# Softmax of the router on 128 partitions, norms two to four units later, another order of the mixers in chunk 0

## What is computed

```python
x = x + _layernorm(_L0_attn_ref(_layernorm(x), a_params, B_w, C_w, D))
x = x + _layernorm(_L0_ffn_ref(_layernorm(x), w_router, w_gating, w_gate, w_up, w_down))

# _L0_attn_ref: Bu = u B_w^T; h = causal convolution of Bu with eig**t, |eig| = 1 (by FFT); y = h C_w^T + D u
# _L0_ffn_ref:
router_probs = softmax(x w_router)
gate_weights = softmax(x w_gating / 0.1)
g, u = x w_gate[e], x w_up[e]          # e = 0..7, 128 -> 512
expert_out = (silu(g) * u) w_down[e]   # 512 -> 128
cw = router_probs * gate_weights
cw = cw / (sum(cw) + 1e-9)
out = sum over e of expert_out[e] * cw[e]
```

## Time and profile before

| | |
|---|---|
| median of 3 runs | 1156.24 us (1155.15 to 1158.2) |
| profiled execution, its time | 1157.83 us |
| profiled execution, its span | 1156.0 us |
| PE, PE weight loads | 1111.9, 898.4 us busy (96%, 78%) |
| DVE | 952.7 us (82%) |
| ACT | 735.2 us (64%) |
| POOL | 721.6 us (62%) |
| DMA | 80.17 MB, mean 69 GB/s |
| granted TensorE clock, mean | 0.996 |

### The profile page before, as it was taken

The page is one execution under the profiler, slowest core; times in us unless marked ns, Lnnn a source line. Parts: engine busy times, 40 slices in busy tenths (PEclk is TensorE's granted clock), DMA queues, the critical chain, the costliest instruction groups (busy, mean ns, idle before and its releaser), DMA issues.

```text
span 1156.0 us, 16762 instructions
## 1 busy us (share of the span) xinstructions
PE 1111.9 (96%) x4818; PEld 898.4 (78%) x4818; DVE 952.7 (82%) x1655; ACT 735.2 (64%) x1415; POOL 721.6 (62%) x900
## 2 busy tenths in 40 slices
PE   7799999999999999999999999999999999999997
PEld 4677787877878778787877878778787877878785
DVE  7778888798898978888897888978888798887865
ACT  6666665756666576675756667576666656656554
POOL 1477765758567475765748566485765748566453
PEclk9999999999999999999999999999999999999998
DMA  4430322313132122322213132222312313132110
GB/s 135 117 101 19 95 62 71 76 46 93 45 92 74 51 79 47 101 56 74 74 46 100 39 93 73 64 67 51 97 55 74 82 39 101 37 83 55 40 53 19
DMA packets 184588, 80.17 MB, mean 69 GB/s; under 512 B 126736, under 2 KB 162224, under 8 KB 184496
## 3 DMA queue, kind: packets, MB, share of 16 engines
q1 hardware_dynamic: 184496, 79.09, 25.7%
HBM read 59.40 MB, written 19.66 MB: 68 GB/s over the span
## 4 chain that ended last, share of the span: by engine, by line
PE 70%; POOL 14%; issue 7%; DVE 7%; ACT 1%; DMA 1%; SPq 0%; POOLq 0%; DVEq 0%; ACTq 0%
PE y L362 8%; PE g L362 7%; PE g L364 7%; PE g L363 7%; PE y L364 7%; PE y L363 7%; PE u L362 7%; PE u L364 7%; PE u L363 7%; POOL hid_lo L1276 6%; POOL acc L1283 3%; DVE e_pos L908 2%; POOL rstd L1248 1%; DVE hid L974 1%; DVE y_part L989 1%
## 5 line engine op out<-in xcount | busy, mean ns | idle before, releaser
L1276 POOL TENSOR_TENSOR hid_lo<-hid,hid_hi 128x512 fp32r<-128x512 f32 x255 | 342.1, 1342 | 338.4 <-ACT hid_hi L670 338.3
L664 ACT ACTIVATE gate<-g 128x512 f32<-128x512 f32 x512 | 304.8, 595 | 325.3 <-PE g L364 325.3
L974 DVE TENSOR_TENSOR hid<-gate,u 128x512 f32<-128x512 f32 x512 | 346.9, 678 | 158.9 <-ACT gate L664 138.4
L670 ACT ACTIVATE hid_hi<-hid 128x512 fp32r<-128x512 f32 x512 | 319.9, 625 | 51.9 <-DVE hid L974 48.1
L980 DVE TENSOR_TENSOR hid_lo<-hid,hid_hi 128x512 fp32r<-128x512 f32 x257 | 237.3, 923 | 0.3
L362 PE MATMUL y<-hid_hi,w_hi 128*128 128x512 f32 x512 | 201.2, 393 | 14.0 <-POOL hid_lo L1276 13.9
L362 PE MATMUL u<-xe_hi,w_hi 128*128 128x512 f32 x512 | 201.4, 393 | 11.4 <-DVE hid L974 11.4
L362 PE MATMUL g<-xe_hi,w_hi 128*128 128x512 f32 x512 | 200.0, 391 | 0.1
L364 PE MATMUL u<-xe_hi,w_lo 128*128 128x512 f32 x512 | 199.6, 390 | 0.0
L364 PE MATMUL y<-hid_hi,w_lo 128*128 128x512 f32 x512 | 199.6, 390 | 0.0
L363 PE MATMUL u<-xe_lo,w_hi 128*128 128x512 f32 x512 | 199.6, 390 | 0.0
(11 more groups left out here) (223 smaller groups left out, 1192.2 us busy)
## 6 DMA issues: line engine op xcount, KB each, us to landing
cw_b<-cw_scratch SPq DMA_DIRECT2D x128, 256.0 KB, 3.4
x_sb<-x_in SPq DMA_DIRECT2D x16, 256.0 KB, 3.1
xn_scratch<-mix_t SPq DMA_DIRECT2D x60, 64.0 KB, 2.7
feat<-xn_scratch SPq DMA_DIRECT2D x15, 256.0 KB, 2.6
out_scratch<-acc_t SPq DMA_DIRECT2D x60, 64.0 KB, 1.9
ffn<-out_scratch SPq DMA_DIRECT2D x15, 256.0 KB, 2.7
x_out<-o_sb SPq DMA_DIRECT2D x15, 256.0 KB, 2.2
y_scratch<-mix_t SPq DMA_DIRECT2D x56, 64.0 KB, 1.9
```

What stands on the lines that cost most here:

```text
L664: nc.scalar.activation(gate[:, k % 2, :], g_ps[k % 2][:], ACT.Silu).then_inc(gate_ready, 1)
L670: nc.scalar.activation(hid_hi[:, k % RING, :], hid[:, k % RING, :], ACT.Copy).then_inc(hi_ready, 1)
L974: nc.vector.tensor_tensor(hid[:, k % RING, :], gate[:, k % 2, :], u_ps[k % 2][:], ALU.mult).then_inc(hid_ready, 1)
L1276: nc.gpsimd.tensor_tensor(hid_lo[:, k % RING, :], hid[:, k % RING, :], hid_hi[:, k % RING, :].bitcast(f32), ALU.subtract).then_inc(lo_pool, 1)
```

## The change

The four tables and a new one for chunk 2's mixers in chunk 0 (`SECOND_X_AT`) move steps between units. In the steady chunks x's first half is two units earlier up to `bu`, y's norm and `z` two units later, the final norm two later. The softmax's tiles have 128 partitions and 4 groups of tokens (128x64 for 32x256). A 32x32 transposition stays within its partitions' block or moves to another; four instructions put the four quarters of the row onto the four blocks of partitions, and four put them back. `lo_x` on DVE waits for `act_hi`, not for `du` that follows it on ACT. In chunk 0 the store of x's blocks goes ahead of `store_cw`, and chunk 1's silus run in chunk 1's unit 0.

```diff
-X_AT = {"load_x": 0, "stats_x": 6, "norm_x": 7, "scale_x_a": 9, "scale_x_b": 10, "block_x": 12, "hi_x": 17, "du": 18,
-        "lo_x": 18, "bu": 20, "enter": 21, "scan": 22, "leave": 23, "hi_w": 25, "lo_w": 26, "c": 28, "y": 29, "block_y": 30}
-Y_AT = {"stats_y": 4, "norm_y": 5, "z_a": 7, "z_b": 8, "residual": 9, "stats_x1": 14, "norm_x1": 15, "scale_x1_a": 17,
...
+X_AT = {"load_x": 0, "stats_x": 4, "norm_x": 5, "scale_x_a": 7, "scale_x_b": 8, "block_x": 10, "hi_x": 15, "du": 16,
+        "lo_x": 16, "bu": 18, "enter": 19, "scan": 21, "leave": 22, "hi_w": 24, "lo_w": 25, "c": 27, "y": 28, "block_y": 30}
+Y_AT = {"stats_y": 6, "norm_y": 7, "z_a": 9, "z_b": 10, "residual": 11, "stats_x1": 14, "norm_x1": 15, "scale_x1_a": 18,
...
-FIN_AT = {"fin_turn": 7, "fin_stats": 10, "fin_norm": 11, "fin_a": 20, "fin_b": 21, "fin_add": 23}
+FIN_AT = {"fin_turn": 7, "fin_stats": 12, "fin_norm": 13, "fin_a": 21, "fin_b": 22, "fin_add": 23}
...
-        lg, e_neg, e_pos = (sb(n, [SMALL, SEQ // SMALL, 2, E]) for n in ("lg", "e_neg", "e_pos"))
+        lg, e_neg, e_pos = (sb(n, [P, NT, 2, E]) for n in ("lg", "e_neg", "e_pos"))
...
             def body(c, par, first, last):
                 if c + 2 < NCHUNK:
                     load_x(c + 2)
+                if first:
+                    store_x_blocks(1)
                 store_cw(c, par)
+                if first:
+                    load_x_feat(1)
                 for e in range(E):
                     spread_cw(c, par, e, first)
-                    if first and e == 0:
-                        store_x_blocks(1)
-                        load_x_feat(1)
...
             def mix_lo_x(c):
-                dve.wait_ge(du_ready, c + 1)
+                dve.wait_ge(act_hi_ready, 2 * c - 1)
...
             def mix_softmax_in(c):
                 dve.wait_ge(logits_ready, c + 1)
-                nc.vector.transpose(sum_sb[0:SMALL, :], n_ps[0:SMALL, :]).then_inc(raw_read, 1)
+                for q in range(P // SMALL):
+                    last = nc.vector.transpose(sum_sb[q * SMALL:(q + 1) * SMALL, 0:P], n_ps[0:SMALL, q * P:(q + 1) * P])
+                last.then_inc(raw_read, 1)
...
-                nc.vector.transpose(cw_t[:], v_sb[0:SMALL, :]).then_inc(cw_t_ready, 1)
+                for q in range(P // SMALL):
+                    last = nc.vector.transpose(cw_t[:, q * P:(q + 1) * P], v_sb[q * SMALL:(q + 1) * SMALL, 0:P])
+                last.then_inc(cw_t_ready, 1)
```

More of the change, by code:

```diff
@@ new lines @@
+Y_AT = {"stats_y": 6, "norm_y": 7, "z_a": 9, "z_b": 10, "residual": 11, "stats_x1": 14, "norm_x1": 15, "scale_x1_a": 18,
+        "scale_x1_b": 19, "block_xe": 20, "hi_xe": 25, "lo_xe": 26, "logits": 28, "softmax": 29, "peak": 30, "silus": 31}
+FIRST_X_AT = {"scale_x_a": 0, "scale_x_b": 1, "block_x": 1, "hi_x": 7, "du": 8, "lo_x": 8, "bu": 10, "enter": 11, "scan": 11,
+              "leave": 13, "hi_w": 14, "lo_w": 14, "c": 16, "y": 17}
+FIRST_Y_AT = {"turn_y": 17, "stats_y": 17, "norm_y": 18, "z_a": 20, "z_b": 21, "residual": 22, "stats_x1": 23, "norm_x1": 24,
+              "scale_x1_a": 26, "scale_x1_b": 27, "turn_xe": 28, "hi_xe": 28, "lo_xe": 28, "logits": 29, "softmax": 30,
+              "peak": 31}
@@ L53 @@
+SECOND_X_AT = {"stats_x": 5, "norm_x": 6, "scale_x_a": 9, "scale_x_b": 10, "block_x": 12, "hi_x": 19, "du": 20, "lo_x": 20,
+               "bu": 21, "enter": 22, "scan": 22, "leave": 23, "hi_w": 25, "lo_w": 26, "c": 28, "y": 29, "block_y": 30}
 OWN_AT = {"exps": 0, "products": 1, "weights": 2}
 FIRST_OWN_AT = {"exps": 1, "products": 1, "weights": 2}
-FIN_AT = {"fin_turn": 7, "fin_stats": 10, "fin_norm": 11, "fin_a": 20, "fin_b": 21, "fin_add": 23}
+FIN_AT = {"fin_turn": 7, "fin_stats": 12, "fin_norm": 13, "fin_a": 21, "fin_b": 22, "fin_add": 23}
@@ L58, in stages @@
 def stages(b):
     if b == 0:
-        return [(1, FIRST_X_AT), (1, FIRST_Y_AT), (2, X_AT)]
+        return [(1, FIRST_X_AT), (1, FIRST_Y_AT), (2, SECOND_X_AT)]
     return [(c, at) for c, at in ((b + 1, Y_AT), (b + 2, X_AT)) if c < NCHUNK]
@@ L717, in body @@
                         mix_silus(0)
+                    if c == 1 and k == 0:
+                        mix_silus(1)
                     for m, at in stages(c):
@@ L930, in mix_weights @@
                 dve.wait_ge(soft_link, at + 2)
-                wide_rows = v_sb[0:SMALL, :].rearrange("p (j q) -> p j q", q=SMALL)
+                wide_rows = v_sb[:, 0:P].rearrange("p (j q) -> p j q", q=SMALL)
                 nc.vector.tensor_tensor(wide_rows[:, :, 0:E], pr[:], wide(den[:], E), ALU.mult).then_inc(cw_ready, 1)
```

9 lines of the change are left out of this document (4 added, 5 removed).

## The result

The changed kernel takes 1148.72 us, the median of four runs (1147.37 to 1149.3), against 1156.03 for the kernel before (1155.15 to 1158.2), measured in turn with it. The ratio is 0.9932, with an interval of 0.9915 to 0.9950. That is 7.3 us less where 27.2 were forecast, and the time lies outside the range of 1119 to 1142. The profiled execution took 1147.37 us, its span was 1145.4.

What follows compares the result with a forecast made beforehand. PE, busy 96% of the span, was taken as the bound, so only its waits could go. 12.6 + 14.1 - 3.0 - 2.0 + 5.5 = 27.2 us off 1156.24 gave 1129.0 us, range 1119 to 1142.

Steps and rivals of the forecast that it cites:

- Loss A: Unit 4, chunks 1 to 15: PE loses 0.84 us waiting for DVE's hid behind the softmax; 12.6 us go.
- Loss B: Unit 8, chunks 1 to 14: PE loses 1.01 us to POOL's queue; goes with Loss A, 14.1 us.
- The cover of the transpositions: Between hid 2 and hid 3: three more transpositions cost PE nothing; without cover 0.2 to 0.4 us a chunk.
- Rival 2: POOL's queue stays the bound, a 1.0 us wait returns at unit 10 or 18 in 13 chunks: 1139; chance 0.17.
- Rival 4: Transpositions far above 1.1 us or DVE late otherwise; Loss A and Loss B stay: 1153; chance 0.04.
- the three signs of being wrong: A wait stays at unit 4; 1 us at Loss B's place or later; PE waits at unit 18 behind feat.
- The 3.0 us of new small waits: New waits from POOL's tight queue in steady chunks: 0.23 us in each of 13; bounds 0 and 1.0 a chunk.
- The feature load: Unit 15: ACT stands 1.5 us or more for feat, just covered at PE's unit 18; 2.0 us over all chunks.
- rival 3: Feature load late in every chunk, each us costing PE one; at 2.6 us late, 1163, slower; chance 0.03.
- Chunk 0: Chunk 0 gives 2.0 us at unit 4, 2.4 at unit 9 and 1.1 right behind; together 5.5 us.
- the two terms: Chunk 0: unit 9's wait for act_lo gives 2.4 us, the lower clock right behind it 1.1.
- The later waits: Chunk 0: later waits for POOL, 3.7 us, change place; taken as equal, 3 us either way.

Runs made afterwards that it cites:

- softmax_only: Kernel before with the softmax alone on 128 partitions, all tables of units as they were; 1146.69 us, ratio 0.9906.
- tables_only: Changed kernel with the softmax back on 32 partitions, the new order of the mixers kept; 1165.04 us, ratio 1.0081.
- quarter_back: Changed kernel with one of the four transpositions of mix_weights, the other three left out and their weights constant; 1135.86 us, ratio 0.9820.
- one_input_products: Changed kernel with pr and den formed by a multiplying reduction that reads one operand; 1141.21 us, ratio 0.9868.
- both_cures: Changed kernel with x's stages up to leave as before, y's statistics at unit 2, its norm and mix_weights at unit 3; 1130.07 us, ratio 0.9771.
- chunk0_as_before: Changed kernel with chunk 0's tables, SP's order there and chunk 1's silus as before; 1148.56 us, ratio 0.9926.
- weights_unit3: Changed kernel with mix_weights in unit 3 instead of 2, behind hid of unit 3; 1148.40 us, ratio 0.9939.
- products_unit0: Changed kernel with mix_products in unit 0 instead of 1, behind mix_exps; 1147.42 us, ratio 0.9926.

## Why the prediction was wrong

**Loss A** was right in place, reason and size: the reciprocal of 128x64 takes 0.545 us (0.54 forecast), `hid` of unit 2 starts 1.47 us earlier in the chunk ("at least 1.2"; the 2.3 called more likely was missed by the 0.98 that `den` took more), and 12.6 us went. softmax_only and tables_only show that it is the softmax alone.

**Loss B** is the step that failed, with some 13 of the 14.1 us that it was to give. The sentence was "Those of `mix_weights` stand behind `hid` 2 and ahead of `hid` 3, which gained at least 1.2 us too, so they cost PE nothing", and after it "With A gone the chain ends at 17.37". To be on time POOL had to start 2.0 us earlier in the chunk than before (12.25 to 10.25, of which that part had 0.2 to spare), so `hid` 3 had to gain some 1.8 to 2.0, not "at least 1.2". It gained 0.99. Two terms took the rest. The transpositions were taken at 0.9 us and took 1.24, above the upper bound of 1.1, since each takes 0.30 and the next starts only behind it. The estimate from the Trainium skill, "VectorE: DVE Perf Modes", section on the TRN2 errata, 0.47 us for three more, was nearer: 1.24 less 0.70 is 0.54. And `den` takes 1.13 us instead of the 0.15 of before, a meeting with POOL that the prediction named for `pr` and did not follow to its neighbour. Taking away either alone (0.93 us by quarter_back, 0.98 by one_input_products) removes nearly all of the wait at unit 8: each is enough, because only the last 1.02 us count. The cover of the transpositions was checked against PE's wait for `hid`, and not against POOL, which hangs on the same `hid`.

None of the rivals gives the measured time. Rival 2 (1139) was right that POOL's queue stays the bound, but had B come back at a later unit, at a cost of 10 us; B never left. Rival 4 (1153) was right in part of its reason, transpositions above 1.1 us (1.24, not "far more") and DVE late for another reason, but had A stay too. Of the three signs of being wrong two came true, 1 us in B's place and a wait at unit 18.

**The 3.0 us of new small waits** did not appear in the change, where B hides them; they appear as 3.6 us in one_input_products, where POOL's chain is still 0.4 us late, and not in quarter_back, where it is on time (with three transpositions left out). both_cures, without them and with all the work, shows that they are a matter of order.

**The feature load** was right as a mechanism and undersized: 2.0 us forecast, 6.1 in the trace. I took the spread of the landing (2.4 to 3.7 us) and no spread for the four stores before it. The load is issued 4.2 us after the first store in the quiet chunks (4.22 in chunk 3, which loses nothing), but 5.4 to 6.1 in chunks 2, 4, 9, 11 and 13, which lose 0.7 to 1.6 each: of the 1.2 to 1.9 us by which the load is issued late, PE loses all but 0.3 to 0.4, close to the one for one of rival 3. That rival's own case, a late load in every chunk, didn't come; without the gain of A the same tables are slower than before, by 9 us between the medians and 6.6 between the spans (tables_only).

**Chunk 0** gave 2.8 us where 5.5 were forecast, and in the four other traces of the same chunk 0 between 1.2 and nothing. Units 9 to 11, with the clock back at full rate, gave 3.9, a little more than the 3.5 of the two terms. Unit 4 gave 1.0, half of the 2.0 (the wait is 1.63 us, was 2.64); with `block_x` behind, in chunk0_as_before, it gave 1.6. The later waits, taken as equal with 3 us either way, cost 1.7 more here. The forecast gave no price to the clock behind a new pause; behind the 2.9 us of unit 28 it is what makes the difference between the traces.

By terms: 14.1 - 3.0 - 1.0 = 10.1 us of B and the new waits, 6.1 - 2.0 = 4.1 of the load and 2.7 of chunk 0 make 16.9 of the 19.7 us between forecast and median. The other 2.8 lie between the profiled executions and the medians: the spans are 10.6 us apart, the medians 7.3 (7.5 from the 1156.24 that the forecast started from).

## What to carry to other kernels

When a stall is to go because its cause goes, compute how much earlier every consumer of the late result must be, not only the one that stalls: here DVE's gain freed PE at once, and POOL's queue, which hangs on the next result and needed about 2 us, got 0.9 and kept the other loss. If a queue with no slack is fed by two late inputs, moving one work item moves the lateness to the other input (weights_unit3, products_unit0); what helped was to let the queue do the long independent item while its inputs are late anyway. A tiny elementwise operation with two SBUF operands is not tiny beside a long POOL instruction; a reduction over the pair does the same arithmetic with one operand.
